# A mixture-of-experts layer: one shared half's products set between the two parts of the second experts, and result gathers without spacing

## The reference, cut to what matters

```python
h = silu(einsum('nd,ehd->neh', flat, gate_w)) * einsum('nd,ehd->neh', flat, up_w)
expert_out = einsum('neh,edh->ned', h, down_w)
sel = take_along_axis(expert_out, topk_idx[:, :, None], axis=1)          # four experts a token
out = (sel * topk_scores[:, :, None]).sum(axis=1)                        # "the expert sums"
out = out + silu(flat @ sgate_w.T) * (flat @ sup_w.T) @ sdown_w.T        # the shared expert
x = layernorm(x + out)
```

## Time and profile before

| | us |
|---|---|
| median of 3 runs | 1230.62 |
| lowest, highest | 1230.23, 1234.17 |
| the profiled execution | 1231.11 |
| its span in the trace | 1229.4 |
| PE busy | 954.5 (78%) |
| DVE busy | 797.2 (65%) |
| ACT busy | 545.4 (44%) |
| POOL busy | 490.1 (40%) |

### The profile page before, as it was taken

The page is one execution under the profiler, slowest core; times in us unless marked ns, Lnnn a source line. Parts: engine busy times, 40 slices in busy tenths (PEclk is TensorE's granted clock), DMA queues, the critical chain, the costliest instruction groups (busy, mean ns, idle before and its releaser), DMA issues. The chain is left out here.

```text
span 1229.4 us, 21000 instructions
## 1 busy us (share of the span) xinstructions
PE 954.5 (78%) x7024; PEld 550.9 (45%) x7024; DVE 797.2 (65%) x2147; ACT 545.4 (44%) x878; POOL 490.1 (40%) x484
## 2 busy tenths in 40 slices
PE   5774116990479989998989998888889979997992
PEld 3563014770223323343333333332278868874552
DVE  3856780004387879779998889979356524555654
ACT  1332003440307756776667575555653424431142
POOL 4011045425632620254006440343544545456775
PEclk8995557996659989999999999988799989999995
DMA  4224202432311210121012222052166746641122
GB/s 120 69 69 134 59 1 67 120 91 45 71 55 43 93 33 29 43 91 37 29 46 63 87 82 81 32 168 100 54 181 197 211 138 172 169 124 50 46 75 66
DMA packets 113331, 105.80 MB, mean 86 GB/s; under 512 B 17854, under 2 KB 95294, under 8 KB 112588
## 3 DMA queue, kind: packets, MB, share of 16 engines
q1 hardware_dynamic: 74108, 65.14, 17.7%
q0 software_dynamic: 12048, 25.71, 7.8%
q10 hardware_dynamic: 27072, 13.64, 3.9%
HBM read 59.60 MB, written 41.55 MB: 82 GB/s over the span
## 5 line engine op out<-in xcount | busy, mean ns | idle before, releaser
L2234 DVE TENSOR_REDUCE maxima<-psum 128x1 f32<-128x512 f32 (+3 forms) x640 | 374.9, 625 | 53.9 <-PE psum L2042 52.0
L2172 ACT ACTIVATE probs<-psum 128x1024 f32<-128x1024 f32 (+3 forms) x384 | 294.5, 810 | 184.7 <-PE psum L2062 182.5
L2042 PE MATMUL psum<-ka,qa 61*128 61x512 bf16 (+3 forms) x768 | 218.4, 351 | 8.0 <-DVE maxima L2234 6.9
L2062 PE MATMUL psum<-qa,ka 64*128 64x512 bf16 (+3 forms) x768 | 169.1, 340 | 4.3 <-ACT probs L2172 3.7
L2077 PE MATMUL psum<-probs,v_wide 128*32 128x512 f32 (+3 forms) x1536 | 169.7, 515 | 0.7 <-ACT outT L2143 0.6
L1541 POOL DMA_INDIRECT sorted<-x_rows,to_row x76 | 75.9, 999 | 189.1 <-DVE to_row L1696 96.5
L2588 ACT ACTIVATE g_silu<-psum 128x512 f32<-128x512 f32 x80 | 47.7, 597 | 178.1 <-PE psum L2494 105.7
L2040 PE MATMUL psum<-mask 64*128 64x128 bf16 x512 | 100.9, 232 | 32.9 <-DMA qa<-max_parts 13.6
L1467 POOL DMA_INDIRECT w_gu<-expert_out,to_row x64 | 66.2, 1034 | 121.5 <-ACT probs L2172 81.7
L2042 PEld LDWEIGHTS psum<-ka,qa 61*128 61x128 bf16 x768 | 68.3, 98 | 92.1 <-DVE maxima L2234 71.7
L2494 PE MATMUL psum<-w_gu,g_xT 128*128 x384 | 97.8, 399 | 8.9 <-DVE g_h L2664 5.4
(11 more groups left out here) (326 smaller groups left out, 1601.6 us busy)
## 6 DMA issues: line engine op xcount, KB each, us to landing
g_rows<-sorted SPq DMA_DIRECT2D x192, 64.0 KB
expert_out<-g_y ACTq DMA_DIRECT2D x48, 256.0 KB
w<-in_W SPq DMA_DIRECT2D x16, 256.0 KB, 3.1
w_gu<-in_gu SPq DMA_DIRECT2D x4, 1024.0 KB, 10.7
sorted<-blank SPq DMA_DIRECT2D x54, 64.0 KB
qa<-q_steps SPq DMA_DIRECT2D x30, 96.0 KB
ka<-k_steps SPq DMA_DIRECT2D x30, 96.0 KB
expert_out<-ey SPq DMA_DIRECT2D x8, 320.0 KB, 3.8
```

Source lines behind the costliest of these rows:

```text
L2042: mm = pe.matmul(bank[:, h * width:(h + 1) * width], qa[b][at:at + ROWS_MAX, (h0 + h) % PER_SIDE, qt * P:(qt + 1) * P], ka[b][at:at + ROWS ...
L2062: mm = pe.matmul(B[score_bank(h)][:, 0:(c + 1) * HALF - q0], ka[s.buf][at:at + ROWS_ALL, h % PER_SIDE, j * P:(j + 1) * P], qa[s.buf][at:at ...
L2172: act.activation(probs[k % PRING][:, 2 * pair:2 * pair + 2, 0:w], PS[:, 2 * pair:2 * pair + 2, 0:w], ACT.Exp).then_inc(exps, 1)
L2234: dve.tensor_reduce(maxima[:, seg, h0:h0 + heads, qt], bank[:, 0:heads * width].rearrange("p (h k) -> p h k", h=heads), AX.X, ALU.max).the ...
```

## The change

Five things, in the words of the code:

- Half 0 of the shared expert (`BETWEEN = 0`) leaves the row of halves behind group 47. Its four chunks stand between the last pieces of group 23, alternating with the down products of groups 22 and 23, and its out products (`emit_out(BETWEEN)`) stand on PE behind the products of group 24. On ACT the three stores of part 0's last groups stand behind the silus of these chunks.
- DVE writes half 0's output, added to the layer's input rows, into `acc` before the expert sums (`add_out(BETWEEN, G.x_rows)`), and the sums of half 0 add onto `acc`; its moments follow its second sum, behind group 32.
- All gathers are issued straight; the waits of `Spaced` are gone for the 64 gathers of halves 0 to 3, which now count on the semaphores that DVE waits for.
- The sums of halves 0 to 2 stand behind groups 29, 32, 35, 39, 42 and 45: six sums beside groups instead of five. The later ones are moved by some chunks.
- The units that count `h_done`, `gu_psum` and `silu_done` are renumbered, so that the four chunks have numbers 24 to 27 and group n of part 1 has n + 4.

```diff
-SUMS_BESIDE_GROUPS = {31: (0, 0), 35: (0, 1), 38: (1, 0), 41: (1, 1), 45: (2, 0)}
-SUMS_BESIDE_CHUNKS = {(0, 1): (2, 1), (1, 0): (3, 0), (2, 0): (3, 1), (2, 3): (4, 0),
-                      (3, 3): (4, 1), (4, 3): (5, 0), (5, 3): (5, 1), (6, 3): (6, 0), (7, 3): (6, 1)}
+SUMS_BESIDE_GROUPS = {29: (0, 0), 32: (0, 1), 35: (1, 0), 39: (1, 1), 42: (2, 0), 45: (2, 1)}
+SUMS_BESIDE_CHUNKS = {(1, 0): (3, 0), (1, 3): (3, 1), (3, 0): (4, 0),
+                      (3, 3): (4, 1), (4, 3): (5, 0), (5, 3): (5, 1), (6, 3): (6, 0), (7, 2): (6, 1)}
+BETWEEN = 0
...
                     if n in PART_ENDS:
                         emit_y(n - 2)
+                        pe.wait_ge(F.loaded, 3 * 16)
+                        pe.wait_ge(F.xT_here, 2 * LAST * 16)
                         emit_hT(n)
+                        emit_chunk(BETWEEN, 0)
                         emit_y(n - 1)
+                        emit_chunk(BETWEEN, 1)
                         emit_y(n)
+                        emit_chunk(BETWEEN, 2)
+                        emit_chunk(BETWEEN, 3)
+                    if n - 1 in PART_ENDS:
+                        emit_out(BETWEEN)
                     if n + 1 < GROUPS:
                         emit_xT(n + 1)
...
-                for i in range(HALVES):
+                for i in range(BETWEEN + 1, HALVES):
                     for c in range(HC1):
                         emit_chunk(i, c)
...
                     if n in SUMS_BESIDE_GROUPS:
                         emit_sums(*SUMS_BESIDE_GROUPS[n])
+                        if SUMS_BESIDE_GROUPS[n] == (BETWEEN, 1):
+                            emit_moments(BETWEEN)
...
-                    if i < PACED_HALVES:
-                        gathers.start(**transfer)
-                    else:
-                        here = tile_landed[t] if i == HALVES - 1 else pair_landed[i % GOT_RING][t // 2]
-                        pool.indirect_dma_start(oob_is_err=False, **transfer).then_inc(here, 16)
+                    here = tile_landed[t] if i == HALVES - 1 else pair_landed[i % GOT_RING][t // 2]
+                    pool.indirect_dma_start(out=got[i % GOT_RING][:, t, k, :], out_offset=None, in_=G.expert_out1[i // BATCH],
+                                            in_offset=bass.IndirectOffsetOnAxis(ap=G.dense1[:, at, k:k + 1], axis=0),
+                                            bounds_check=PART_TILES * P - 1, oob_is_err=False).then_inc(here, 16)
```

More of the change, by code:

```diff
@@ L2372, in stage_experts1 @@
                                            for name in ("var_eps", "less_mean", "rstd", "shift")]
-        landed, got_landed = [M.sem(f"landed{u}") for u in range(AHEAD1)], [M.sem(f"got_landed{u}") for u in range(AHEAD_GOT)]
+        landed = [M.sem(f"landed{u}") for u in range(AHEAD1)]
         pair_landed = [[M.sem(f"pair_landed{v}_{q}") for q in range(2)] for v in range(GOT_RING)]
@@ L2621, in _ @@
                         copy_hT(n)
-                        for m in range(n - 2, n + 1):
-                            store(m)
+                        emit_chunk_silu(chunk_unit(BETWEEN, 0))
+                        store(n - 2)
+                        emit_chunk_silu(chunk_unit(BETWEEN, 1))
+                        store(n - 1)
+                        emit_chunk_silu(chunk_unit(BETWEEN, 2))
+                        store(n)
+                        emit_chunk_silu(chunk_unit(BETWEEN, 3))
                     if n == EXP_AT:
@@ L2639, in _ @@
                 store(GROUPS - 3)
-                for i in range(HALVES):
+                for i in range(BETWEEN + 1, HALVES):
                     for c in range(HC1):
-                        emit_silu(chunk_unit(i, c))
-                        if i == 0 and c < 2:
+                        emit_chunk_silu(chunk_unit(i, c))
+                        if i == BETWEEN + 1 and c < 2:
                             store(GROUPS - 2 + c)
@@ L2687, in emit_sums @@
                                                             scalar=G.gate1[:, at, k:k + 1],
-                                                            in1=acc[:, at, :] if k else G.x_rows[:, at, :], op0=ALU.mult, op1=ALU.add)
+                                                            in1=acc[:, at, :] if k or i == BETWEEN else G.x_rows[:, at, :],
+                                                            op0=ALU.mult, op1=ALU.add)
                         if k < K1 - 1:
@@ L2758, in _ @@
                     if n in PART_ENDS:
-                        for m in range(n - 2, n + 1):
-                            emit_y(m)
+                        emit_y(n - 2)
+                        emit_chunk(BETWEEN, 0)
+                        emit_y(n - 1)
+                        emit_chunk(BETWEEN, 1)
+                        emit_y(n)
+                        emit_chunk(BETWEEN, 2)
+                        emit_chunk(BETWEEN, 3)
+                    if n - 1 in PART_ENDS:
+                        add_out(BETWEEN, G.x_rows)
                     if n < TABLE_AT:
@@ L2769, in _ @@
                         emit_sums(*SUMS_BESIDE_GROUPS[n])
+                        if SUMS_BESIDE_GROUPS[n] == (BETWEEN, 1):
+                            emit_moments(BETWEEN)
                 queue.drain()
                 emit_y(GROUPS - 2)
-                for i in range(HALVES):
+                for i in range(BETWEEN + 1, HALVES):
                     for c in range(HC1):
                         emit_chunk(i, c)
-                        if c == 0 and i == 0:
+                        if c == 0 and i == BETWEEN + 1:
                             emit_y(GROUPS - 1)
```

60 lines of the change are left out of this document (30 added, 30 removed).

## The result

| | before | after |
|---|---|---|
| median, us | 1231.93 (14 runs, 1225.88 to 1236.3) | 1223.79 (14 runs, 1213.17 to 1232.95) |
| ratio to before, 95% interval | | 0.9924 [0.9901, 0.9946] |
| profiled execution, us | 1231.11 | 1224.42 |
| its span, us | 1229.4 | 1222.7 |

By the ratio the kernel is 0.76% faster, with an interval of 0.54 to 0.99%; the two medians lie 8.1 us apart, 0.66%. The ratio leaves out one slow run of the changed kernel, 1232.95 us. The forecast, 1219.5 beside 1230.62, is a ratio of 0.9910 and lies in the interval; the median lies in the range forecast.

The account below looks back on a forecast made before the run. POOL's spaced gathers were taken as the bound; part 1's last store at 1105.92 + 1.7 + 0.43 + 1.73, gathers 3.57 later, 11.14 us earlier than before: span 1218.3, median 1219.5, range 1213.5 to 1226.5 (0.83).

Parts of the forecast that it names:

- The bound: POOL's spaced part-0 gathers delay part 1's; straight, they take 1.31 us each and POOL idles some 20 us until part 1's store.
- The switch, +1.7: Between the parts on PE: half 0's four chunks and out products delay group 25 by 1.7 us, bounds -1.8 to 10.45.
- The sums, +0.43 and +1.73: DVE beside part 1's groups: a sixth sum holds PE 0.43 us, half 0's moments 1.73; together 0 to 4.3.
- The stretch: Time from group 23's transposes of `g_h` (995.51) to part 1's first gather, forecast at 1113.35.
- Behind group 47: Seven shared halves instead of eight: some 11 us of PE work leave, worth nothing; the 104.91 us to the end stay.
- the tail: Time from part 1's first gather to the end of the span: forecast to stay at 104.91 us.
- The time: Forecast span 1218.3 us, 1220.0 in a profile, median 1219.5 against 1230.62.
- One, traffic: Straight gathers take the loads' DMA share, groups wait for rows: 1224.5 to 1229 us, chance 0.08; in full 1236, 0.05.
- Two, the queue: The queue, not the waits, holds part-0 gathers at 1.88 us each: median 1234.0, chance 0.05.
- Three, the shared halves as the bound: Seven shared halves behind group 47 at 15.4 us each end last instead of the gathers: 1224 to 1229 us, chance 0.05.

Follow-up runs that it names:

- cut sums: Changed kernel with each sum beside groups cut into two times four instructions behind two groups, half 0's moments behind group 36: 1217.2 us (0.9861 of before), again 1214.97 (0.9857).
- straight gathers alone: Kernel before with `Spaced` taken out of the result gathers, all eight halves still behind group 47: 1225.28 us, 0.9936 of before.
- late out products: Changed kernel with half 0's out products, DVE add and moments back behind group 47, part 1's last store moved earlier: 1221.67 us, 0.9900 of before.
- three gathers in flight: Kernel before with gather u waiting for gather u-3, one number changed; not timed, two profiles: 107.61 and 113.74 us from group 23's transposes to part 1's first gather.

## Why the prediction was right, point by point

*The bound.* Right. The spaced gathers were what part 1's first gather waited for; without spacing it waits for the last store, and POOL stands idle 22.77 us (forecast: some 20).

*The switch, +1.7.* Right for the profile on which it rests. Group 25 was to come 17.8 us behind group 23's transposes (1013.3 against 995.51) and came at 1018.16 - 1000.84 = 17.32; group 24 took 1.99 as forecast. What I did not see is that the idle time filled here is no fixed number. Against the second profile of before, where PE waited 1.31 us and group 25 came at 11.86, the half between the parts costs 5.5. That +1.7 fits is in part owed to which execution of before had been profiled.

*The sums, +0.43 and +1.73.* Right: 0.43 behind each sum, and 2.35 behind the one with the moments, against 0.43 + 1.73 = 2.16. Cut in two and moved, as the kernel with cut sums shows, all of it was to be had back.

*The stretch.* 1113.35 - 995.51 = 117.84 forecast, 117.31 measured.

*Behind group 47.* The number, 104.91, was right (104.55), and its reason was wrong: this is the step that failed. I wrote that the 11 us of PE work that leave the row are worth nothing, since POOL's gathers end last. That holds for seven halves, and with 4.9 us to spare: I had the row end near 1184 and the last tile land at 1208.9. The row took 90.5 us from its first chunk, not 78. One half took 16.8 instead of the steady 11.21 (out products at 1132.17 and 1148.97), with a wait of 3.07 for `s_hT` and a granted clock of 0.66 from 1140 to 1150; and the last half's out products wait (3.88) and take 5.44 instead of 3.57:

```profile
1195.35 5.44 PE L2530 MATMUL psum<-sd_sb,s_hT 128*128 128x128 f32 x32 [3.88 <-DVE acc L2714]
```

With eight halves and straight gathers the tail is 113.6. So in the tail the work that left is worth about 8.7 us; in the stretch it costs, 117.31 and 119.33 against 113.62 and 110.40. That the forecast of 104.91 held is owed to a margin that it did not work out. The trace of before already showed how small that was. There the first and the last of the last four tiles were:

```profile
1208.87 0.35 DVE L2714 SCALAR_TENSOR_TENSOR acc<-f_got,gate,x_rows 128x128 f32<-128x128 f32 x1 [4.89 <-PE psum L2526]
...
1220.10 0.35 DVE L2714 SCALAR_TENSOR_TENSOR acc<-f_got,gate,x_rows 128x128 f32<-128x128 f32 x1 [2.55 <-DMA f_got<-expert_out,dense]
```

The first waited for out products, and at 2.79 us a tile the row of eight halves would have let the last begin at 1217.24, only 2.9 us ahead of where its landing put it; by the same working it is 7.3 and 3.1 us in the other two profiles of before, and 6.9 in the second of the changed kernel. Gathers of part 1 that come 15 us earlier bring the end forward by as much only if that row ends earlier too.

*The time.* Stretch and tail were forecast at 222.75 and measured at 221.86. The profiled execution came out at 1224.42 instead of 1220.0, which the 5.33 us of the later start account for. The median of 1223.79 stands beside one of 1231.93 for before; scaled to that, the forecast is 1220.8, a gain of 11.1 us where the medians show 8.1 and the ratio 9.4.

*The rivals.* One, traffic: the estimate of a DMA share of 0.68 was met by 0.69, and the groups kept their 3.74 us; PE waits for no rows in part 1, and the gathers land within 2.8 us of their issue, where the longest took 4.9 before. The Trainium skill, "DMA: Bandwidth & Descriptors", section "Queues, rings and completion order", has the engines take queues with work in turn; a third queue that is always filled would by this hold up the loads, and at this share nothing of it shows. Two, the queue: fell, 1.31 each. Three, the shared halves as the bound: did not happen in the changed kernel, but lies 4.9 us away, and happens when work of half 0 is put back into the row under straight gathers (straight gathers alone, late out products). Its 0.05 looks low beside that margin.

## What to carry to other kernels

When a list on one engine is the bound, work out for the next engine behind it not how long its work is but when it ends, waits and slow stretches included: here two lists ended 3 to 7 us apart, and speeding up the one alone took 15.4 us off the stretch and gave 8.7 back in the tail. Small work that is put beside a busy engine costs the piece that exceeds the slack in each slot, so cut it to the slot's size: here that brought 0.7%, about as much as the change itself (0.8%). Before an idle time is counted as a gain to be filled, look at it in more than one execution.

## What was not expected of the hardware

PE's idle time at the switch between the parts, for the kernel before, was 4.57, 1.31 and 4.45 us in three executions; group 24 behind it took 3.77, 3.31 and 3.59 us, and 1.99 with three gathers in flight in the execution where PE did not wait for rows. Behind a wait of 2.35 us in the middle of the groups the products ran at full clock in one execution and, in another, took 2.92 instead of 1.99, with a granted clock of 0.89 from 1060 to 1070.
